# A Mamba block with a routed MLP on one core: the order of PE, ACT, POOL and VectorE in the scan loop's front half

## What is computed

```
h    = layernorm(layernorm(x)) * norm_w + norm_b          # 256 channels
h    = silu(causal_conv4(h @ in_proj_w.T))                # 512 channels
proj = h @ x_proj_w.T                                     # 1 + 16 + 16 rows: dt_in, B, C
dt   = softplus(dt_in * dt_proj_w + dt_proj_b)
state[n] = exp(-exp(A_log)[n] * dt) * state[n] + B[n] * h # scan over 512 positions, 16 states
y    = sum_n state[n] * C[n] + D * h
x1   = x + layernorm(silu(y) @ out_proj_w.T + layernorm(x))
```

## Time and profile before

| | |
|---|---|
| median of 3 runs | 1407.54 us |
| the profiled execution | 1406.39 us |
| its span | 1404.6 us |
| mean granted TensorE clock | 0.947 |
| busy: PE, VectorE, POOL, ACT | 84%, 77%, 76%, 57% of the span |
| start of scan 0 of iterations 0 to 7 | 50.6, 172.5, 290.9, 407.2, 523.3, 639.4, 755.5, 871.6 us |
| from one to the next | 121.86, 118.43, 116.29, 116.13, 116.11, 116.09, 116.05 us |
| last scan ends | 984.5 us |
| from DMA issue to landing (median): cbc, bbc | 4.7, 6.2 us |

### The profile page before, as it was taken

One profiled execution on the slowest core, in us unless ns is written; L12 is line 12 of the kernel. 1 busy time (PEld: TensorE's weight loads), 2 busy tenths in 40 slices (PEclk: granted clock), 3 DMA queues, 4 the chain that ended last, 5 costly groups with the idle time before them and its releaser, 6 DMA issues.

```text
span 1404.6 us, 15181 instructions
## 1 busy us (share of the span) xinstructions
PE 1174.1 (84%) x4798; PEld 517.3 (37%) x4799; DVE 1085.5 (77%) x1403; ACT 795.9 (57%) x1379; POOL 1072.3 (76%) x557
## 2 busy tenths in 40 slices
PE   5657878787797986988778687788999999999996
PEld 2212223222332422322233142233556656566653
DVE  4588998999999899999999989799241115776675
ACT  5757668777877777877786686645431111111111
POOL 0579999999999999999999999999123814544553
PEclk9889999998998999999999998899999999999998
DMA  3921211240250132123024013200279422222220
GB/s 108 282 61 62 91 60 32 75 150 1 77 180 1 62 112 83 32 82 143 3 79 161 0 63 142 83 1 31 90 251 318 159 73 82 80 80 79 86 63 15
DMA packets 72067, 127.65 MB, mean 91 GB/s; under 512 B 8759, under 2 KB 48448, under 8 KB 67904
## 3 DMA queue, kind: packets, MB, share of 16 engines
q1 hardware_dynamic: 60432, 103.72, 22.2%
q0 software_dynamic: 7152, 16.81, 3.8%
q10 hardware_dynamic: 4416, 6.29, 1.3%
HBM read 97.79 MB, written 31.76 MB: 92 GB/s over the span
## 4 chain that ended last, share of the span: by engine, by line
PE 41%; DVE 19%; POOL 19%; ACT 13%; issue 5%; DMA 1%; DVEq 0%; POOLq 0%; ACTq 0%; SPq 0%
POOL state L515 11%; DVE state L1123 11%; PE psX L1678 10%; POOL bx L504 6%; PE psX L1613 5%; PE psY L1560 4%; ACT psX L789 4%; PE psY L1626 3%; DVE acc L1058 3%; DVE bx L1111 3%; PE bank L1517 3%; PE psY L1695 2%; PE bank L1695 2%; POOL lt L520 2%; PE bank L1450 2%
## 5 line engine op out<-in xcount | busy, mean ns | idle before, releaser
L515 POOL TENSOR_TENSOR state<-state,cbc 128x1024 f32<-128x1024 f32 x256 | 606.0, 2395 | 9.9 <-DVE state L1123 9.9
L1123 DVE TENSOR_TENSOR_SCAN state<-psX,bx 128x1024 f32<-128x1024 f32 x256 | 581.3, 2283 | 27.9 <-ACT psX L789 20.4
L789 ACT ACTIVATE psX<-dt,aneg 128x511 f32<-128x511 f32 x512 | 330.7, 680 | 128.6 <-DVE state L1123 128.5
L504 POOL TENSOR_TENSOR bx<-xh,bbc 128x1024 f32<-128x1024 f32 x112 | 273.0, 2438 | 75.8 <-DMA bbc<-bc_rows 41.8
L1560 PE MATMUL psY<-state,ident 64*64 64x512 f32 x2048 | 285.6, 644 | 35.9 <-POOL state L515 35.5
L1517 PE MATMUL bank<-prow,ident 128*128 128x512 f32 x288 | 175.7, 695 | 113.1 <-DVE bx L1111 113.1
L1111 DVE TENSOR_TENSOR bx<-xh,bank 128x1024 f32<-128x1024 f32 x144 | 172.8, 1200 | 22.4 <-PE bank L1517 22.1
L1560 PEld LDWEIGHTS psY<-state,ident 64*64 64x64 f32 x2048 | 61.2, 137 | 221.7 <-issue 117.2
L994 ACT ACTIVATE sg<-psX 128x512 f32<-128x512 f32 x39 | 23.3, 597 | 196.7 <-PE psX L1678 191.4
L1517 PEld LDWEIGHTS bank<-prow,ident 128*128 128x128 f32 x288 | 51.2, 209 | 211.6 <-DVE bx L1111 172.3
L585 POOL DMA_INDIRECT ysl<-shared_rows,idx x39 | 40.4, 1036 | 80.4 <-DVE idx L1289 75.7
(11 more groups left out here) (207 smaller groups left out, 1725.5 us busy)
## 6 DMA issues: line engine op xcount, KB each, us to landing
cbc<-bc_rows SPq DMA_DIRECT2D x32, 1024.0 KB, 4.7
bbc<-bc_rows SPq DMA_DIRECT2D x16, 1024.0 KB, 6.2
slot_in<-ao SPq DMA_DIRECT2D x1, 5011.5 KB, 34.8
xsl<-slot_in SPq DMA_DIRECT2D x39, 128.5 KB
xin<-in_x SPq DMA_DIRECT2D x8, 512.0 KB, 5.1
xr<-in_x SPq DMA_DIRECT2D x8, 512.0 KB, 5.9
x_rows<-ao SPq DMA_DIRECT2D x8, 512.0 KB, 2.9
xn_rows<-xr SPq DMA_DIRECT2D x8, 512.0 KB, 3.3
```

The lines of the kernel that those rows point to most:

```text
L504: nc.gpsimd.tensor_tensor(bx[q % RB][:], xh[par][:, h * CH:(h + 1) * CH], bbc[:, n // 2].unsqueeze(1).broadcast_to([P, CH, L]), ALU.mult). ...
L515: nc.gpsimd.tensor_tensor(w[:], w[:], cbc[:, n].unsqueeze(1).broadcast_to([P, CH, L]), ALU.mult).then_inc(weighted, 1)
L789: e = nc.scalar.activation(decay[q % RD][:, c, 1:L], dt[par][:, h * CH + c, 1:L], ACT.Exp, scale=aneg[:, h * CH + c, n:n + 1])
L1123: nc.vector.tensor_tensor_scan(st[q % RS][:].rearrange("p c t -> p (c t)"), decay[q % RD].rearrange("p c t -> p (c t)"), bx[q % RB][:].rea ...
```

## The change

Line numbers of what follows are those of the diff. It moves instructions to other steps, and alters the waits that guard the bank psF accordingly:

- dt's row on PE from step 11 to 10, z on ACT from 12 and 13 to 11 and 12.
- B and C on PE from step 14 to 18, behind both adds of the projection out of the same iteration (new wait on `ao_done`); their copy `prow` on ACT from 14 to 19. The first projection out of step 15 now waits for z instead of prow, and `choose` waits for prow.
- VectorE's two adds of the projection out from 17 and 19 to 16 and 18 (in all iterations, the statistics with them).
- |z| 14 to 13, exp 15 to 14, 1 + u 16 to 15, difference 17 to 16, logarithm 19 to 17, Square 22 to 20, ReLU 23 to 22 on ACT; the loss on POOL 20 to 18; min() on VectorE from 23 and 24 to 21 and 23.

```diff
--- before.py
+++ after.py
@@ -527,7 +527,7 @@
                         elif do_front:
                             inject(i + 1, 1 - par, q + RB - Q)
                     weigh(i, q)
-                    if do_front and q == 20:
+                    if do_front and q == 18:
                         loss(i + 1, 1 - par)

             for q in range(0, RB, 2):
@@ -684,35 +684,36 @@
                     if not (isinstance(f, int) and f < 2):
                         act.wait_ge(y_kept, H * (f - 1))
                     nc.scalar.activation(xh[par][:], acc[:], ACT.Silu).then_inc(xh_ready, 1)
-                if q in (12, 13):
+                if q in (11, 12):
                     act.wait_ge(dtin_ready, f + 1)
                     act.wait_ge(xh_ready, f + 1)
-                    for c in (0, 1) if q == 12 else (2, 3):
+                    for c in (0, 1) if q == 11 else (2, 3):
                         last = nc.scalar.activation(acc[:, c], psF[:], ACT.Identity,
                                                     scale=dtw[:, c:c + 1], bias=dtb[:, c:c + 1])
-                    if q == 13:
+                    if q == 12:
                         last.then_inc(z_done, 1)
-                if q == 14:
+                if q == 19:
                     act.wait_ge(proj_ready, f + 1)
                     nc.scalar.activation(prow[par][:], psF[:], ACT.Identity).then_inc(prow_kept, 1)
+                if q == 13:
                     act.wait_ge(z_done, f + 1)
                     nc.scalar.activation(tmp[:], acc[:], ACT.Abs).then_inc(sf, 1)
-                if q == 15:
+                if q == 14:
                     act.wait_ge(sf, 2 * f + 1)
                     nc.scalar.activation(tmp[:], tmp[:], ACT.Exp, scale=-1.0).then_inc(u_ready, 1)
-                if q == 16:
+                if q == 15:
                     act.wait_ge(u_ready, f + 1)
                     nc.scalar.activation(lt[:], tmp[:], ACT.Identity, bias=1.0).then_inc(sf, 1)
-                if q == 17:
+                if q == 16:
                     act.wait_ge(sf, 2 * f + 2)
                     nc.scalar.activation(lt[:], lt[:], ACT.Identity, bias=mone[:]).then_inc(lt_ready, 1)
-                if q == 19:
+                if q == 17:
                     act.wait_ge(lt_ready, f + 1)
                     nc.scalar.activation(dt[par][:], lt[:], ACT.Ln, bias=1.0).then_inc(soft_ready, 1)
-                if q == 22:
+                if q == 20:
                     act.wait_ge(loss_ready, f + 1)
                     nc.scalar.activation(dt[par][:], tmp[:], ACT.Square, scale=HALF_ROOT).then_inc(sq_ready, 1)
-                if q == 23:
+                if q == 22:
                     nc.scalar.activation(acc[:], acc[:], ACT.Relu).then_inc(relu_ready, 1)
                 if q in (25, 26, 27, 28):
                     c = q - 25
@@ -1063,23 +1064,23 @@
                             last.then_inc(conv_done, 1)
                         else:
                             cf.link(f, last)
-                if q in (23, 24):
-
-
-                    h = slice(0, 2) if q == 23 else slice(2, 4)
+                if q in (21, 23):
+
+
+                    h = slice(0, 2) if q == 21 else slice(2, 4)
                     dve.wait_ge(loss_ready, f + 1)
                     dve.wait_ge(sq_ready, f + 1)
                     nc.vector.scalar_tensor_tensor(out=lt[:, h], in0=lt[:, h], scalar=LN_MARGIN, in1=dt[par][:, h],
                                                    op0=ALU.add, op1=ALU.min).then_inc(min_done, 1)

             def back(b, q):
-                if q in (17, 19):
+                if q in (16, 18):
                     h = q // 2 - 8
                     dve.wait_ge(h0_ready, b + 1)
                     dve.wait_ge(oproj_ready, 2 * b + h + 1)
                     half = ao[:, 2 * h:2 * h + 2].rearrange("p a c -> p (a c)")
                     nc.vector.tensor_tensor(half, psF[:], half, ALU.add).then_inc(ao_done, 1)
-                if q == 19:
+                if q == 18:
                     dve.wait_ge(ao_done, 2 * b + 2)
                     stats(1, cb, b, ao, mv[1], mv_ready[1])
                 if q in (22, 24):
@@ -1199,9 +1200,9 @@

             sh_act(0, 0, 0)
             sh_act(0, 0, 1)
-            back(NB - 1, 17)
+            back(NB - 1, 16)
             sh_act(0, 0, 2)
-            back(NB - 1, 19)
+            back(NB - 1, 18)
             sh_act(0, 0, 3)
             choose(NB - 2)
             back(NB - 1, 22)
@@ -1437,15 +1438,17 @@
                         last = nc.tensor.matmul(psF[:], win[:, k, c * P:(c + 1) * P], hT[:, k],
                                                 start=(k == 0), stop=(k == KC - 1))
                     last.then_inc(inproj_ready, 1)
-                if q == 11:
+                if q == 10:
                     pe.wait_ge(xh_ready, f + 1)
                     pe.wait_ge(conv_done, C * (f + 1))
                     for c in range(C):
                         last = nc.tensor.matmul(psF[:], xp[:, c, 0:1].broadcast_to([P, P]), xh[par][:, c],
                                                 start=(c == 0), stop=(c == C - 1))
                     last.then_inc(dtin_ready, 1)
-                if q == 14:
+                if q == 18:
                     pe.wait_ge(z_done, f + 1)
+                    if f >= 2:
+                        pe.wait_ge(ao_done, 2 * (f - 1))
                     for c in range(C):
                         last = nc.tensor.matmul(psF[:], w_bc[:, c].rearrange("p g r -> p (g r)"), xh[par][:, c],
                                                 start=(c == 0), stop=(c == C - 1))
@@ -1472,7 +1475,7 @@
                     if h == 1:
                         pe.wait_ge(ao_done, 2 * b + 1)
                     elif do_front:
-                        pe.wait_ge(prow_kept, b + 3)
+                        pe.wait_ge(z_done, b + 3)
                     elif b == NB - 2:
                         pe.wait_ge(e_act, FC)
                     else:
@@ -1500,7 +1503,9 @@

             def choose(b):
                 pe.wait_ge(xnT_copied, KC * (b + 1))
-                if b < NB - 1:
+                if b < NB - 3:
+                    pe.wait_ge(prow_kept, b + 4)
+                elif b < NB - 1:
                     pe.wait_ge(ao_done, 2 * (b + 2))
                 for j in range(J):
                     for k in range(KC):
```

## The result

The changed kernel has a median of 1433.26 us (1430.55 to 1439.18, 4 runs) against 1408.01 us (1406.61 to 1409.23, 4 runs) for the kernel before on the same chip: a ratio of 1.0185, 95% interval 1.0151 to 1.022. The forecast was 1415, its range 1401 to 1424. The profiled execution took 1430.55 us, its span is 1428.7, the mean granted clock 0.942. Scan 0 of the iterations starts at 50.6, 179.3, 295.4, 417.3, 534.1, 656.2, 772.9 and 895.1 us, the last scan ends at 1008.8.

A forecast was written before the change was run, and what follows sets the result against it. It took VectorE's inject of 25, which releases PE's gapless 19.3 us from spread(27), to set the period, not POOL, the fullest engine. 6 x 1.1 + 0.5 + 0.7 = +7.8 on the median 1407.54 gave 1415, range 1401 to 1424.

The forecast's parts named there:

- c: Both min() on VectorE: each waits out the rest of POOL's current instruction; +1.3 us a period, bounds 0 to 4.6.
- Rival 3: First min() arrives just after weigh(20) starts and waits 2.3; +1.5 to +2.5 more a period, near 1425; chance 0.10.
- dt's row in step 10: On PE between spread(12) and spread(13): VectorE's inject of 13 comes later, +3.4 us a period, bounds +3.0 to +3.9.
- The waits that go: VectorE's waits before injects 15 and 17 and scan 17 vanish: -3.2 us a period, or -2.4.
- the adds: Output projection's two VectorE adds in steps 16 and 18, each now following an inject: -0.5 us, bounds -0.6 and 0.
- POOL: weigh(13) waits 1.7, the loss fills the former gap, weigh(21) starts 1.5 sooner; counts only if POOL sets the end.
- Rival 1: POOL sets the period: -1.5 x 6 = -9, 1398.5, or -19 if weigh(13) isn't late; chance 0.20.
- min() ahead of the inject of 25: Both min(), steps 21 and 23, now precede VectorE's inject of 25, making it later by +1.1 us.
- What inject 25 sets: Inject 25 ends 2.1 later, PE's 19.3 us from spread(27) do not shrink; +1.3 a period, 1.1 taken.
- Queues: SP's store of B and C's rows moves from step 14 to 19, choose() waits for prow: costs nothing.
- Ends: First and last iterations: iteration 0 some +0.5 us (0 to +2), last iteration +0.7.
- Rival 2: The mins meet no POOL instruction (c = 0): period 1.3 less, total 1407.5; chance 0.22.

The follow-up runs named there:

- e13: Changed kernel plus a one-column POOL memset ahead of each of weigh(20) to weigh(23); 1408.63 us, ratio 1.0009.
- e3: Changed kernel with min() replaced by two statistics instructions reading lt alone, one SBUF operand, the bound left out; 1407.15 us, ratio 0.9999.
- e6: Changed kernel with POOL held by a semaphore ahead of weigh(20) until the first min() is done; 1416.47 us, ratio 1.0063.
- e16: Control: changed kernel with e13's four memsets placed ahead of weigh(2) to weigh(5), far from min(); median 1431.81 us.
- e1: Changed kernel with min() back in steps 23 and 24; 1441.41 us, ratio 1.023.
- e9: Kernel before the change with min() one step later, in 24 and 25; 1420.6 us, ratio 1.011.
- e4: Changed kernel with the two dt buffers exchanged in memory; 1432.63 us, ratio 1.0178.
- e12: Changed kernel with the halves exchanged, first min() on chunks 2 and 3, second on 0 and 1; 1427.92 us, ratio 1.0137.
- e15: e1 (min() back in steps 23 and 24) plus POOL memsets ahead of weigh(22) to weigh(25); 1423.01 us, ratio 1.0125.
- e14: Changed kernel with dt's row split over steps 10 and 11, softplus a step later, min() in 23 and 24, memsets ahead of weigh(21) to weigh(24); 1411.83 us.
- e2: Changed kernel with dt's row back in PE's step 11 and z in 12 and 13; 1423.27 us, ratio 1.0094.
- e11: Changed kernel with four one-column memsets on VectorE ahead of the first min(); median 1428.66 us.
- e5: Changed kernel with e2 and e3 together: dt's row in step 11, one-operand instructions for min(); 1405.35 us, ratio 0.9979.
- e7: Kernel before the change with e3's one-operand instructions for min(), in steps 23 and 24; 1405.23 us, ratio 0.9981.
- e10: Changed kernel with min() in 24 and 25, POOL held ahead of weigh(23) and weigh(24) until each is done; 1408.13 us, ratio 1.0016.

## Why the prediction was wrong

**The step that failed** is the term c, "two SBUF operands": "each min waits for what is left of POOL's instruction, 0 to 2.3". It counted on one POOL instruction. In the changed kernel four of the seven first min() were passed by the instructions queued behind that one too, and had their turn only when POOL had none left: three of 6.34 to 6.38 and one of 8.25. Rival 3 had the mechanism (the first min() misses its turn) but priced it with the same bound, at 2.3, and so stopped near 1425. The mistake was in reading one row for a rule: the 14 instances held only wins, so they could bound the wait of a winner and nothing else. The rule of the Trainium skill (SBUF — State Buffer, Who interferes with whom) that I set beside it, that the two exclude each other instruction by instruction in issue order, does not cover this either, and the measurement decides: min() had been issued 0.6 before POOL's weigh(20) could start, and weigh(20) and weigh(21) went ahead of it.

Its size is more than the whole miss of 18 us. Iteration 0 takes 128.7, where e13, without a passed min(), takes 124.21 and e3 122.15; iterations 2, 4 and 6 take 121.91 to 122.16 where 3 and 5 take 116.7: 5.2 + 5.4 + 5.4 and 4.5 to 6.6 are 20.5 to 22.6 us, and the profiled execution's 1430.55 less that is 1408 to 1410. That the wait is the cause is shown from three sides: the two-operand instruction gone (e3, 1407.15), POOL held (e6, 1416.47), the memset in place (e13, 1408.63) against the memset elsewhere (e16, 1431.81).

**The other terms**, in the short period of iteration 3:
- *dt's row in step 10*, +3.4: right. It took 4.52 for my 4.15, 0.4 more, and the inject of 13 waited 3.56, within the bounds of 3.0 and 3.9.
- *The waits that go*, -3.2, and *the adds*, -0.5: right. Scan 20 follows scan 13 by 21.84 where I had 22, with no wait between.
- *POOL*: right. It idles 2.45 ahead of weigh(13) where I had 1.7, none before the loss, and its -1.5 was worth nothing: Rival 1 fell. POOL has 5.9 to spare in the short period (116.74 less 110.88), more than before.
- *min() ahead of the inject of 25*, +1.1, and c where min() wins, +1.3: right. The two take 1.73 and 1.90, 0.53 and 0.70 of it waiting; from scan 20 to spread(27) it is 20.63 (490.22 to 510.85) against 18.28, +2.35 for my 2.4. The first did come 0.6 before POOL's next start, as reckoned.
- *What inject 25 sets*: nearly twice too dear. "Its 19.3 us without a gap do not shrink": they shrank, to 18.58 (510.85 to 529.43). The granted clock in the first 5 us of that stretch was 0.50 before and is 0.66 now:

```profile
499.35:504.35 5.00, 5.00 (x12) 1.37 (x13) 5.00 (x5) 2.69 (x10) 5.00 (x3) 0.50 0.31 107
```

```profile
510.85:515.85 5.00, 5.00 (x13) 1.31 (x14) 4.96 (x12) 2.84 (x10) 5.00 (x3) 0.66 0.73 256
```

  The first row is of the kernel before, the second of the changed one. The low level of 1.2 GHz ends sooner in it (spread(27) itself takes 1.78 for 2.08), although PE had idled 3.50 for 3.33 before. From scan 0 on, scan 20 is 1.03 sooner (72.87 for 73.90; I had 0.3 and the absorbed 0.79), spread(27) 2.36 later by that, and the stretch 0.75 shorter: +0.58, where I had +1.1. In e13 the period is 116.05 to 116.13, that of before. Without passed min() the change is worth 0 to +0.6 a period.
- *Queues*: right, nothing: in the loop POOL never waits for a load of `bbc` or `cbc`. *Ends*: the last iteration +0.8 for +0.7; iteration 0 without a passed min() has +0.3 to +2.4 (e3, e13) for +0.5, iteration 1, for which I had +1.1, gives 2.3 back. Without the passed min() the sum is 5 x 0.6 - 2.3 + 0.8 and the 0.3 to 2.4 of iteration 0, so +1.8 to +3.9 for my +7.8.

By this count the case that I forecast, every min() having its turn, is worth 1408.63 (e13), not 1415. That e6 lands on 1416.5 is no confirmation: it adds a wait of 1.16 on POOL that my sum did not have. Rival 2's 1407.5 is near that too, but not for its reason: c was not 0, each min() waited 0.5 or more.

**What stays open.** What decides whether min() has its turn. It is not its step (e1, e9), the buffer (e4), the half (e12), or its distance from POOL's next start: at 0.6 us it both wins and loses, within one execution. That the number of losses differs between executions of one kernel is inferred from their times (1407.54 to 1450.79 in e16), as one of each was traced. It is not a POOL instruction without reads in between alone, as e15 loses two in seven with it. In the profiled runs with the memset in place (e13, e14, e15) 18 of 21 first min() were not passed; in the changed kernel, e1 and e16, without it, 7 of 21, and with e2, e4, e11 and e12 counted too, 20 of 49. Not one second min() was passed in any of them, and I have no reason for that.

That no arrangement's median fell below 1405 is open too: the steady period is 116.05 to 116.17 in before, e3, e5 and e13 from iteration 3 on, and 116.01 to 116.06 in e14, though they gain and lose up to 2.4 on the way. It is not a floor for a single period (115.47 in e7, 115.45 in e10, 115.52 in e15). I saw for e13 where it is made up (PE's stretch from spread(27), 18.5 for 19.3), not why it ends so alike.

## What to carry to other kernels

An exclusion between two engines that each hold the access for one instruction was not bounded here by one instruction: the one that waits may be passed for as long as the other has work queued. So price a rare two-operand instruction on VectorE beside a full POOL queue by the time until POOL runs dry, and look at its longest instance, not at its mean. Where a long instance shows, try the cheap remedies first: one SBUF operand fewer, a semaphore that holds the other engine, or an instruction without reads in its queue. Here they were worth 17 to 26 us of 1433, and at best brought the change back to the time of the kernel before. And a kernel whose runs spread by 2% with most terms of its profile unchanged may hold such a draw: take more runs before a verdict.

## What the runs showed of the hardware that I had not expected

- A waiting VectorE instruction with two SBUF operands was passed by two to four whole POOL instructions of 2.3 us each (6.34 to 8.25 us in the changed kernel, 11.12 in e1), in e2 also by one, for 1.2 of own work.
- When it wins, it costs POOL 1.0 (3.3 for 2.36). When it loses, it costs POOL nothing until POOL is dry, and then POOL waits too (3.36 for scan 22).
- Of 20 first min() that were waiting when a POOL instruction of 0.1 us that reads nothing came, 18 had their turn there (e13, e14, e15). Two were passed at two of them each.
- Two instructions that read `lt` alone, one SBUF operand, took 1.28 together at the same moment, undisturbed (e3).
- The length of PE's idling before a stretch does not by itself set the clock in it. In the first 5 us from spread(27), iterations 1 to 6, 0.50 to 0.52 was granted after 3.31 to 3.33 of idling in the kernel before, and 0.66 to 0.69 after 3.29 to 3.44 in e13. In the changed kernel it was 0.66 to 0.67 in the short periods (after 3.28 to 3.53) and 0.50 in the long ones (after 3.44 to 3.55).
